# First stage of a graph-attention kernel: its scores from three merged products, its work ordered in six steps of two heads, its projections over three banks

## What is computed

```python
h = jnp.einsum('bnd,ade->bane', feat_in, W)
th = jnp.tanh(h)
attn_src = jnp.einsum('bane,aeo->bano', th, w_src)
attn_dst = jnp.einsum('bane,aeo->bano', th, w_dst)
attn = attn_src + jnp.swapaxes(attn_dst, 2, 3)
attn = jnp.where(attn >= 0, attn, LEAKY_ALPHA * attn)
mask = ~adj[:, None, :, :]
attn = jnp.where(mask, jnp.float32(-999.0), attn)
attn = jax.nn.softmax(attn, axis=-1)
feat_out = jnp.einsum('banm,bame->bane', attn, h) + b
feat_out = jax.nn.elu(feat_out)          # heads side by side
gate = jax.nn.sigmoid(feat_in @ H_w.T + H_b)
return gate * feat_out + (1.0 - gate) * feat_in
```

## Time and profile before

| | |
|---|---|
| median of 3 runs | 3392.78 us (3390.15 to 3398.41) |
| the profiled execution's own time | 3394.71 us |
| its span, first to last instruction | 3392.9 us |
| busy over the span: PE, DVE, ACT, POOL | 93%, 72%, 61%, 31% |
| granted TensorE clock, mean | 0.993 of full |
| first x of the second phase issued at | 1063.53 us |

### The profile page before, as it was taken

One profiled execution on the slowest core, in us unless ns is written; L12 is line 12 of the kernel. 1 busy time (PEld: TensorE's weight loads), 2 busy tenths in 40 slices (PEclk: granted clock), 3 DMA queues, 4 the chain that ended last, 5 costly groups with the idle time before them and its releaser, 6 DMA issues. The chain is left out here.

```text
span 3392.9 us, 80994 instructions
## 1 busy us (share of the span) xinstructions
PE 3138.5 (93%) x24736; PEld 2633.6 (78%) x24736; DVE 2426.2 (72%) x8331; ACT 2060.1 (61%) x6315; POOL 1055.9 (31%) x1014
## 2 busy tenths in 40 slices
PE   6999999999995999999999999999999999999997
PEld 5777777777774788878888788878888888878886
DVE  4767767767774777777777777777777777777776
ACT  5878788878884555555555555555555555555554
POOL 1333333333333423232322423232323223232323
PEclk9999999999997999999999999999999999999999
DMA  2011001101102111111111111111111011111110
GB/s 71 23 31 32 27 27 32 32 22 32 32 16 72 31 32 42 32 43 31 42 35 38 60 41 37 36 38 36 42 32 42 32 42 37 36 38 36 42 32 30
DMA packets 107121, 123.91 MB, mean 37 GB/s; under 512 B 39680, under 2 KB 106176, under 8 KB 106176
## 3 DMA queue, kind: packets, MB, share of 16 engines
q1 hardware_dynamic: 106688, 118.57, 11.1%
HBM read 68.22 MB, written 50.33 MB: 35 GB/s over the span
## 5 line engine op out<-in xcount | busy, mean ns | idle before, releaser
L835 ACT ACTIVATE a_probs<-a_logits,a_nmax 128x256 f32<-128x256 f32 x1152 | 574.0, 502 | 273.9 <-DVE a_nmax L916 273.9
L774 POOL TENSOR_TENSOR a_residual<-a_x,a_br 128x384 f32<-128x384 f32 x192 | 191.1, 1019 | 1542.1 <-DVE a_mix L944 1528.4
L96 PE MATMUL a_pj<-a_xt_hi,a_w_lo 128*128 128x256 f32 x1728 | 512.7, 297 | 6.1 <-DVE a_xt_lo L901 5.2
L97 PE MATMUL a_pj<-a_xt_lo,a_w_hi 128*128 128x256 f32 x1728 | 484.2, 280 | 0.0
L98 PE MATMUL a_pj<-a_xt_hi,a_w_hi 128*128 128x256 f32 x1728 | 483.9, 280 | 0.0
L466 DVE CUSTOM_DVE_ANT_0 g_v<-g_z,g_v 128x256 f32<-128x256 f32 x768 | 293.3, 419 | 245.3 <-ACT g_v L364 242.4
L916 DVE CUSTOM_DVE_ANT_0 a_logits<-a_s,a_mask 128x256 f32<-128x256 f32 x1152 | 416.6, 417 | 0.8 <-PE a_s L1070 0.5
L937 DVE TENSOR_SCALAR a_probs<-a_probs,a_recs 128x256 f32<-128x256 f32 x1152 | 395.0, 385 | 20.4
L370 ACT ACTIVATE g_exps<-g_v,g_nmax 128x256 f32<-128x256 f32 x768 | 383.9, 509 | 0.9 <-DVE g_nmax L466 0.7
L96 PEld LDWEIGHTS a_pj<-a_xt_hi,a_w_lo 128*128 128x128 f32 x1728 | 325.4, 188 | 33.4 <-issue 5.4
L906 DVE SCALAR_TENSOR_TENSOR a_qk_lo<-a_pj,a_bc,a_qk_hi 128x256 fp32r<-128x256 f32 x576 | 251.1, 477 | 131.0 <-ACT a_qk_hi L828 131.0
(11 more groups left out here) (116 smaller groups left out, 8360.8 us busy)
## 6 DMA issues: line engine op xcount, KB each, us to landing
a_x<-y SPq DMA_DIRECT2D x96, 384.0 KB, 3.1
y<-a_out SPq DMA_DIRECT2D x96, 384.0 KB, 2.5
g_x<-x SPq DMA_DIRECT2D x32, 384.0 KB, 3.0
y<-g_out SPq DMA_DIRECT2D x32, 384.0 KB, 2.5
w_stage<-att_w SPq DMA_DIRECT2D x3, 2304.0 KB, 9.8
a_adj<-adj SPq DMA_DIRECT2D x96, 64.0 KB, 2.8
g_adj<-adj SPq DMA_DIRECT2D x32, 64.0 KB, 2.8
g_w_stage<-gat_w SPq DMA_DIRECT2D x1, 1152.0 KB, 5.6
```

The source lines that it names most:

```text
L96: pe.matmul(out, a[1], b[0], start=first, stop=False)
L97: pe.matmul(out, a[0], b[1], start=False, stop=False)
L835: last = act.activation(probs[:, (HEADS * u + h) % 4, t, :], logits[:, h % 2, t, :], ACT.Exp, scale=-1.0, bias=nmax[:, u, h, t:t + 1], acc ...
```

## The change

Four things in `gat_phase`; `attention_phase` is as it was.

1. The scores of a head are three matmuls: one with 512 columns that writes the mask to both halves, and one a half of 256 columns. For it `z_left` holds ones in its upper 64 rows and the sources' terms in its lower 64, and `z_right` holds for each head the targets' terms above and ones below, both times the head's selecting column. `z_right` is new work: GpSimd multiplies it out each sample, in six instructions of 128x512. The mask is in f32r.
2. Three banks instead of two serve the steps and the backs; `cx` has one instead of two.
3. The rows of the gates' bias product go over all 128 rows instead of 64.
4. All engines' orders are written anew: six steps of two heads, the two heads' transposes together.

```diff
-                            pe.matmul(z, sel_dst[:, j, :], sd[u][:, :], start=True, stop=False)
-                            pe.matmul(z, sd[u][:, t * P:(t + 1) * P], sel_src[:, j, :], start=False, stop=False)
-                            last = pe.matmul(z, ident_bf[:, :], mask[u][:, t, :], start=False, stop=True)
...
+            def scores_of(half, u, h):
+                if h == 0:
+                    pe.wait_ge(mask_ready, at(1, half, u, 1))
+                if h % Z_GROUP == 0:
+                    pe.wait_ge(z_right_done, at(GAT_HEADS // Z_GROUP, half, u, h // Z_GROUP + 1))
+                pe.wait_ge(maxed, at(GAT_HEADS, half, u, h - 1))
+                pe.matmul(z_ps[h % 2][:, :, :], ident_r[:, :], mask[u][:, :, :], start=True, stop=False)
+                for t in range(NT):
+                    last = pe.matmul(z_ps[h % 2][:, t, :], z_left[u][:, t * P:(t + 1) * P], z_right[u][:, h, :], start=False, stop=t == NT - 1)
+                last.then_inc(scores, 1)
...
+            def spread_targets(half, u, prev):
+                if prev:
+                    pool.wait_ge(scores, at(GAT_HEADS, *prev, GAT_HEADS))
+                held(pool, pj_read, reads(half, u, SD), passed)
+                for h in range(0, GAT_HEADS, Z_GROUP):
+                    heads = slice(h, h + Z_GROUP)
+                    shape = [P, Z_GROUP, N]
+                    pool.tensor_tensor(z_right[u][:, heads, :], f32(s_dst[u][:, :]).unsqueeze(1).to_broadcast(shape),
+                                       sel[:, heads].unsqueeze(2).to_broadcast(shape), ALU.mult).then_inc(z_right_done, 1)
...
-        BANK = {X: 0, X + 1: 1, H: 0, H + 1: 0, TT: 1, TT + 1: 0, G: 1, SD: 0, LAST: 1}
+        BANK = {X: 0, X + 1: 1, H: 0, H + 1: 1, TT: 1, TT + 1: 2, G: 1, SD: 0, LAST: 2}
+        BACK_BANK = (2, 0)
...
-        hb_stage, hb_hi, hb = sb("hb_stage", [2 * 32, D]), sb("hb_hi", [2 * 32, D], F32R), sb("hb", [2 * 32, D], F32R)
+        hb_stage, hb_hi, hb = sb("hb_stage", [P, D]), sb("hb_hi", [P, D], F32R), sb("hb", [P, D], F32R)
...
-                if k == SD:
-                    act.activation(sd[u][:, :], ps[:, 0:N], ACT.Identity).then_inc(pj_hi, 1)
...
+            def high_sd(half, u):
...
+                act.activation(z_left[u][SRC, :], ps[SRC, 0:N], ACT.Identity)
+                act.activation(s_dst[u][DST, :], ps[DST, 0:N], ACT.Identity).then_inc(pj_hi, 1)
```

More of the change, by code:

```diff
@@ L106, in gat_phase @@
     STEPS = 9
+    HALF = P // 2
     QUAD = P // GAT_DIM
@@ L118, in gat_phase @@
         adj_sb = [sb(f"adj{p}", [P, NT, N], U8) for p in range(2)]
-        mask = [sb(f"mask{p}", [P, NT, N], BF16) for p in range(2)]
+        mask = [sb(f"mask{p}", [P, NT, N], F32R) for p in range(2)]
         w_stage = sb("w_stage", [P, 2, DC, D])
@@ L358, in slot @@
             def slot(cur, nxt, prev):
[L359 to L392, removed]
@@ L458, in statistics @@
                     dve.bn_aggr(mv[:, t, :], stats[:, t, :]).then_inc(aggr, 1)
-            def slot(cur, nxt, prev):
[L461 to L471, removed]
-                    if prev and j == 9:
-                        elu_and_gate(*prev)
-                    if nxt and PLAN.get(j) in READ_STEPS:
-                        lo_of_step(*nxt, PLAN[j])
-                    head = behind(cur, prev, GAT_HEADS, j, T_LAG)
-                    if head and head[2] % 2 == 1:
-                        half, u, h = head
-                        dve.wait_ge(transposed, at(GAT_HEADS, half, u, h + 1))
-                        dve.wait_ge(contexts, at(GROUPS, half, u, h // QUAD - 1))
-                        dve.tensor_copy(pt_sb[:, pt_slot(u, h)], pt_ps[1][:, :, :]).then_inc(pt_odd_read, 1)
-                    if prev and j == 2:
-                        invert(*prev)
-                    if prev and j == 7:
-                        elu_argument(*prev)
-                    if prev and j == 11:
-                        statistics(*prev)
@@ new lines, in maximum, with odd_pt @@
+            def maximum(half, u, h):
+                held(dve, lrelu, at(GAT_HEADS, half, u, h + 1), passed)
+                for t in range(NT):
+                    last = dve.tensor_tensor_reduce(
+                        out=v_sb[:, h % 3, t, :], in0=z_ps[h % 2][:, t, :], in1=v_sb[:, h % 3, t, :], scale=-1.0,
+                        scalar=BIG, op0=ALU.add, op1=ALU.min, accum_out=nmax[:, u, h, t:t + 1])
+                last.then_inc(maxed, 1)
+            def odd_pt(half, u, pair):
+                dve.wait_ge(transposed, at(GAT_HEADS // 2, half, u, pair + 1))
+                dve.wait_ge(contexts, at(GROUPS, half, u, pair // 2 - 1))
+                dve.tensor_copy(pt_sb[:, pt_slot(u, 2 * pair + 1)], pt_ps[1][:, :, :]).then_inc(pt_odd_read, 1)
@@ new lines, in make_state, with transpose_state @@
+            def make_state(half, u, t):
+                pe.wait_ge(pj_read, reads(half, u, X + t))
+                rows = slice(t * P, (t + 1) * P)
+                for c in range(DC):
+                    last = product(pe, pj_bank(H + t)[:, 0:D], (xt_hi[:, c, rows], xt_lo[:, c, rows]), (w_hi[:, 0, c, :], w_lo[:, 0, c, :]),
+                                   first=c == 0, last=c == DC - 1)
+                last.then_inc(pj_made, 1)
+            def transpose_state(half, u, t):
+                pe.wait_ge(pj_hi, at(len(HI_STEPS), half, u, HI_STEPS[H + 1]))
+                if t == 1:
+                    pe.wait_ge(gate_done, at(NT, half, u, 0))
+                    pe.wait_ge(back_read, at(NT, half, u, 1 - 2 * NT))
+                for c in range(DC):
+                    last = pe.transpose(pj_bank(TT + t)[:, c * P:(c + 1) * P], th[:, t, c * P:(c + 1) * P], ident[:, :])
+                last.then_inc(pj_made, 1)
@@ new lines, in make_sd, with make_gate @@
+            def make_sd(half, u):
+                pe.wait_ge(pj_read, reads(half, u, TT + 1))
+                pe.wait_ge(back_read, at(NT, half, u, -NT))
+                for c in range(DC):
+                    last = product(pe, pj_bank(SD)[:, 0:N], (sd_hi[:, c, :], sd_lo[:, c, :]), (tt_hi[:, c, :], tt_lo[:, c, :]),
+                                   first=c == 0, last=c == DC - 1)
+                last.then_inc(pj_made, 1)
+            def make_gate(half, u, t, chunks):
+                if 0 in chunks:
+                    pe.wait_ge(pj_read, reads(half, u, TT + t))
+                out = pj_bank(LAST if t else G)[:, 0:D]
+                rows = slice(t * P, (t + 1) * P)
+                for c in chunks:
+                    product(pe, out, (xt_hi[:, c, rows], xt_lo[:, c, rows]), (w_hi[:, 1, c, :], w_lo[:, 1, c, :]), first=c == 0, last=False)
@@ L534, in make_step @@
                 if DC - 1 in chunks:
-                    last.then_inc(pj_made, 1)
+                    pe.matmul(out, ones[:, :], hb[:, :], start=False, stop=True).then_inc(pj_made, 1)
             def make_back(half, u, t, cur, nxt):
```

383 lines of the change are left out of this document (263 added, 120 removed).

## The result

The changed kernel took 3218.87 us, median of 4 runs (3218.05 to 3220.02), against 3395.6 for the kernel before beside it: ratio 0.948 with a 95% interval of 0.9465 to 0.9498. That is 177 us less, where the forecast was 151 less. The prediction's range holds it (3205 to 3320); it lies one microsecond under the narrower range of case A (3220 to 3280).

A forecast was written before the change was run, and what follows sets the result against it. PE's 26.1 us plus hand-offs was taken to bound the 31.29 us slot; the new one is ACT's 25.25 + 0.45 + 0.4, plus 0.3: 26.4. Loop slots save 147 us, the rest 4: 3242 us, range 3205 to 3320.

The forecast's parts named there:

- case A: The forecast itself: loop slot 25.7 to 27.6 us, time 3280 to 3220 us; chance 0.64.
- the walk: The new slot followed instruction by instruction from ACT's first Relu: 25.25 + 0.45 + 0.4 = 26.1 us.
- Rival D: Score merging fails: the 512-column matmul costs 0.47 us, PE back at 25.5, slot about 28, 3290 us; chance 0.03.
- the ring: GpSimd's work and products, closed through DVE's minimum and ACT's Exp, elu and gate: 22.6 us with products at 7.7.
- B: GpSimd's ring sets the slot: 29.0 us with products at 13.2, still faster, 3320 us; chance 0.11.
- E: Slower through GpSimd's ring: equals the old slot at 2.6 us per product, 3428 us at 2.8; chance 0.04.
- Exp 10: ACT's Exp in step five: waits 0.4 us, as its minimum follows DVE's elu, gate, copy and SD's lower parts.
- the surcharge of 0.3: Added to the walked slot of 26.1 us for hand-offs rounded away, making 26.4.
- The ends: Outside the loop slots: two other slots with scores save about 3 us each, the opening costs 2; net 4 us.
- The opening: Start of the first phase: pays 2 us for GpSimd's first product and the two hand-offs.
- C: Two heads together make ACT and PE take turns, 0.3 to 0.4 us per step: slot 28.5, 3305 us; chance 0.15.
- F: No change: an overlooked wait takes back just the slot's 5 us; chance 0.03.

## Why the prediction was right, and where it was not

**The destination was read rightly.** "ACT is now the longest engine" and "PE's saving past that is not paid out" hold: the merge's 3.0 us of PE (2.6 as measured below) are worth 1.4, the bias rows' 0.5 are worth 0.12, and taking a wait and two copies from ACT gives time back. Added up from start to start, over four slots, ACT has 24.8 us of work a slot after (forecast 25.25), 96% of the slot, and stands 1.0 us.

**The start was not.** "So the slot is PE's 26.1 us plus hand-offs" failed. It would make each microsecond saved on PE worth one in the old order; the merge was worth 11 us of the 90 forecast on PE (some 80 measured) and the bias rows 6 of 18 (15 measured). The runs put in its place a chain over PE and ACT through two shared banks and ACT's wait for the gated product. The rows priced the banks at 1.8 us a slot, what PE stood there; what they allowed once PE was faster was 66 us, 1.9 a slot, and ACT's 2.1 us in the earlier trace rows was written off as waiting like the rest, though no saving on PE could touch it. The forecast was then right by its other end: before minus the new floor. It did not rest on the wrong reading, since the walk was made from ACT's side.

**The terms.** The scores first. Timeline of PE after, a pair of heads behind the transposes, beside the earlier trace rows:

```profile
422.70 0.48 PE L664 MATMUL g_z<-g_mask,g_ident_r 128*128 128x512 f32 x1
423.02 0.39 PE L666 MATMUL g_z<-g_z_right,g_z_left 128*128 128x256 f32 x2
423.25 0.39 PE L664 MATMUL g_z<-g_mask,g_ident_r 128*128 128x512 f32 x1
423.48 0.39 PE L666 MATMUL g_z<-g_z_right,g_z_left 128*128 128x256 f32 x2
```

The first head of a pair takes 423.25 - 422.70 = 0.55, the second 0.46 (431.17 to 431.63 in the next pair); 0.47 was right for one and 0.08 short for the other, so PE saves some 2.6 us a slot and not 3.0; in the old order its busy time fell by the same 2.6. The 512 columns alone take 0.23 in the second head, as estimated. Rival D is out.

A gate's end beside the earlier trace rows:

```profile
420.08 0.34 PE L98 MATMUL g_pj<-g_w_hi,g_xt_hi 128*128 128x384 f32 x1
420.26 0.33 PE L644 MATMUL g_pj<-g_hb,g_ones 128*128 128x384 f32 x1
420.52 1.07 PE L689 MATMUL g_cx_ps<-g_pt_copy,g_h 128*32 128x256 f32 x16
```

0.44 us before the contexts, 0.35 at the other gate (from 417.87 to 418.22), so 0.29 and 0.20 saved of 0.64 each, 0.49 in all, between the ends given (0.3 and 0.6). The 0.09 that stays stands at the change to 32 columns, where the Trainium skill puts a drain (TensorEngine Tiling (Array Packing), Key Properties). By this trace it costs a third of what going to 64 rows and back did.

GpSimd, its groups in the nine slots and its timeline behind the sum, beside the earlier trace rows:

```profile
L281 POOL TENSOR_TENSOR g_z_right<-g_s_dst,g_sel 128x512 fp32r<-128x512 f32 x54 | 54.3, 1039 | 0.0
...
L293 POOL TENSOR_TENSOR g_cx<-g_cx,g_b 128x384 f32<-128x384 f32 x18 | 18.1, 1008 | 15.1 <-DVE g_cx L502 15.1
```

```profile
420.76 6.04 POOL L281 TENSOR_TENSOR g_z_right<-g_s_dst,g_sel 128x512 fp32r<-128x512 f32 x6
426.76 0.23 POOL L286 TENSOR_SCALAR g_var<-g_mv 128x2 f32<-128x2 f32 x1
```

Six in 6.0 us, the forecast's low bound, not 7.7: 512 elements from repeated operands take 1039 ns in the mean, about as long as 384 from plain ones (1008). GpSimd's work is 17.35 us a slot instead of 19.1. That changes no time, since the ring is 4 us away, and rivals B and E are out.

ACT's copies of the scores' terms, and the copy of h that waits:

```profile
416.90 0.38 ACT L376 ACTIVATE g_z_left<-g_pj 64x256 fp32r<-64x256 f32 x1
417.29 0.38 ACT L377 ACTIVATE g_s_dst<-g_pj 64x256 fp32r<-64x256 f32 x1
417.57 0.50 ACT L356 ACTIVATE g_exps<-g_v,g_nmax 128x256 f32<-128x256 f32 x1
...
429.90 0.49 ACT L371 ACTIVATE g_h<-g_pj 128x384 f32<-128x384 f32 x1 [0.43 <-PE g_cx_ps L689]
```

The pair keeps ACT 0.67 us instead of one copy's 0.26, so it costs 0.4, not 0.26. The wait for the contexts is 0.43 in its forecast place (0.4 to 0.5), and taking it away gave 7 us, so it was real. Exp 10 stood about 0.15 us, not 0.4. A stand of 0.2 us before the first of the two copies was not forecast.

**Where the rest came from.** Between the profiled executions the change took 174.7 us, 24 more than forecast. A slot was 0.58 short of 26.4: ACT's work came out 0.45 lower than forecast, and its standing 1.0 instead of 1.15 (0.45, 0.4 and the surcharge of 0.3). 30 slots make 17 us. The ends gave 178.4 - 30 x (31.29 - 25.82) = 14 us, not 4. The opening was to cost 2 us and the first scores came 5.1 us sooner (33.97 instead of 39.02). The other 9 us, counted between the first scores of the slots: the slot before the loop gave 4.1 (28.09 before, 23.97 after), the last slot with the close of the phase 4.3 (50.88 and 46.60), and the two turns of the loop 0.8 together. The second phase took back 3 us.

**Rivals.** C, taking turns in pairs, did not come: ACT stands 0.7 us a slot by name, and half of that is in two single waits of the nine slots. F is out.

## What to carry to other kernels

A saving on the busiest engine is worth what the engine after it in the loop lets through, so compute the new slot from the next floor up and not from the old slot down. Here PE was busy 92% of the slot and ACT still stood 6 us of 31, and they held each other. In such a case look at each repeated wait of the second engine for one that the edit cannot shorten, here a gate read too early and two banks between nine steps, for these decide whether the saving arrives (11 us or 44 for the same merge). Test a bundle by adding its parts to the old kernel too, not only by taking them out of the new one, since the two give different prices.

## What the runs showed of the hardware

**PE's clock fell behind some waits, and the next slot paid for it.** In the kernel with merged scores and three banks the granted clock was 0.96 over the eight slots, and 1.00 with the late gate. Windows inside one slot, two microseconds each:

```profile
521.00:523.00 2.00, 1.59 (x21) 0.77 (x20) 1.16 (x6) 1.97 (x6) 0.35 (x1) 1.00 0.00 0
523.00:525.00 2.00, 0.52 (x1) 0.49 (x2) 1.74 (x7) 1.83 (x7) 1.69 (x2) 0.88 0.00 0
525.00:527.00 2.00, 2.00 (x11) 1.94 (x10) 1.47 (x7) 1.28 (x4) 2.00 (x3) 0.50 0.00 0
527.00:529.00 2.00, 2.00 (x13) 1.86 (x13) 1.59 (x6) 1.75 (x6) 2.00 (x3) 0.76 0.02 4
529.00:531.00 2.00, 1.59 (x12) 1.30 (x11) 1.91 (x8) 2.00 (x9) 1.71 (x4) 1.00 0.02 4
```

PE stands 1.9 us for GpSimd's first product, until 524.5. Then the grant falls to 1.2 GHz (0.50), and it is back at 2.4 GHz by 529. In the three windows the grant falls short of full speed by 0.24 + 1.0 + 0.48 = 1.7 us. The same wait, 1.9 to 3.1 us long, stands in each of the eight slots, yet five read 0.94 and three 1.00, so the wait by itself does not decide it. Three slots in a row:

```profile
480.12:508.88 28.76, 25.42 (x198) 20.78 (x197) 22.11 (x75) 25.36 (x79) 17.40 (x16) 1.00 0.10 32
508.88:537.65 28.77, 26.15 (x194) 21.69 (x194) 21.63 (x71) 24.82 (x77) 17.40 (x16) 0.94 0.10 31
537.65:567.24 29.59, 27.30 (x203) 22.74 (x201) 22.76 (x79) 26.07 (x83) 17.37 (x16) 0.94 0.10 30
```

The slot in which the clock falls is no longer than the one before it; the one behind it is. Within all three turns of the loop, a slot behind one at 1.00 took 28.73 to 28.82 us, and a slot behind one at 0.94 took 28.90 to 29.59. With full clock throughout the slot would be about 28.75, an estimate from these rows, against the mean of 28.97. So the clock cost 0.2 us a slot, far less than the grant's shortfall of 1.7 us in five slots of eight; that PE stands in the slot anyway would explain it, but is not shown. Of the 1.8 us a slot that the late gate gave, 0.2 are the clock's and 1.6 the waits'.

**The second phase isn't a constant.** Its instructions are the same in all kernels, yet it took 2329.4 us before, 2332.7 after, 2334.0 with merged scores alone and 2336.3 with the order alone, as large as the effect of the bias rows. Each figure is one execution, and runs of one kernel differ by as much (3389 to 3398 us for the one before). For small parts of a phase, its own slots tell more than the program's time.
